# Two graph-attention layers on one core: q's second-layer weights loaded in place through GpSimd, and the first layer's residual loaded one step earlier

## The reference

```python
h = relu(layernorm(x))
q, k, v = h @ Wq + bq, h @ Wk + bk, h @ Wv + bv          # layer 1, 12 heads
p = softmax(where(adj > 0, q @ k.T / sqrt(32) + beta * adj, -9e15))
x = x + p @ v
h = relu(layernorm(x))
q, k, v = h @ Wq1.T, h @ Wk1.T, h @ Wv1.T + bv1          # layer 2
p = softmax(q @ k.T / sqrt(384) + 2 * adj)               # rows of zeros give 0
x = x + (p @ v) @ Wo.T + bo
```

## Time and profile before

| | before |
|---|---|
| median of 3 runs | 1955.08 us (1952.37 to 1955.17) |
| the profiled execution | 1955.73 us, span 1954.0 us |
| TensorE busy | 1900.2 us (97%) |
| VectorE busy | 1819.8 us (93%) |
| ScalarE busy | 1608.5 us (82%) |
| GpSimd busy | 1001.9 us (51%) |
| mean granted TensorE clock | 0.996 |
| chain that ended last | TensorE 63%, VectorE 31% of the span |

### The profile page before, as it was taken

One profiled execution on the slowest core, in us unless ns is written; L12 is line 12 of the kernel. 1 busy time (PEld: TensorE's weight loads), 2 busy tenths in 40 slices (PEclk: granted clock), 3 DMA queues, 4 the chain that ended last, 5 costly groups with the idle time before them and its releaser, 6 DMA issues.

```text
span 1954.0 us, 50144 instructions
## 1 busy us (share of the span) xinstructions
PE 1900.2 (97%) x18396; PEld 1233.7 (63%) x18396; DVE 1819.8 (93%) x3986; ACT 1608.5 (82%) x4150; POOL 1001.9 (51%) x1243
## 2 busy tenths in 40 slices
PE   7999999999999999999999999999999999999999
PEld 5566666666666666666566666666666666666665
DVE  6999999999999999999899999999999999999994
ACT  5899888998988889998878777877778777877785
POOL 6466655566766555665453443434343444344331
PEclk9999999999999999999999999999999999999999
DMA  4888989989989899899887877877887887787774
GB/s 156 210 209 228 224 231 231 236 228 240 229 229 225 230 229 239 230 238 236 219 228 196 215 201 195 212 205 202 203 211 193 214 204 202 203 214 195 202 196 128
DMA packets 104564, 415.94 MB, mean 213 GB/s; under 512 B 27104, under 2 KB 30432, under 8 KB 104320
## 3 DMA queue, kind: packets, MB, share of 16 engines
q1 hardware_dynamic: 77552, 305.11, 64.9%
q0 software_dynamic: 26768, 107.62, 17.3%
HBM read 88.61 MB, written 25.17 MB: 58 GB/s over the span
## 4 chain that ended last, share of the span: by engine, by line
PE 63%; DVE 31%; issue 2%; POOL 1%; ACT 1%; DMA 1%; DVEq 0%; SPq 0%; POOLq 0%
DVE s L432 17%; PE ring L301 15%; PE sc L266 14%; PE out L362 11%; DVE pt L445 11%; PE ring L330 6%; PE ring L283 6%; PE ring L309 5%; PE ring L292 2%; PE ring L332 1%; PE ring L321 1%; DVE stats L491 1%; DVE nmax L432 1%; DMA res<-in_x 0%; DVE oT L483 0%
## 5 line engine op out<-in xcount | busy, mean ns | idle before, releaser
L552 ACT ACTIVATE s<-s,nmax 128x512 f32<-128x512 f32 x1536 | 1095.9, 727 | 197.1 <-DVE nmax L432 196.1
L432 DVE CUSTOM_DVE_ANT_0 s<-sc,bias 128x512 f32<-128x512 f32 x1536 | 968.1, 686 | 57.5 <-PE sc L266 36.0
L445 DVE STREAM_TRANSPOSE pt<-s 128x2048 f32<-128x2048 f32 x285 | 656.9, 2305 | 1.2 <-ACT s L552 1.2
L266 PE MATMUL sc<-k,q 32*128 32x512 f32 x3072 | 439.4, 642 | 39.9 <-DVE nmax L432 36.6
L552 ACT ACTIVATION_READ_ACCUMULATOR s<-s,nmax 128x1 f32 x1536 | 313.2, 204 | 0.0
L362 PE MATMUL out<-pk,v 128*32 128x192 f32 x6080 | 286.5, 329 | 0.0
L362 PEld LDWEIGHTS out<-pk,v 128*32 128x32 f32 x6080 | 178.0, 109 | 135.4 <-issue 98.1
L309 PE MATMUL ring<-wv,hT 128*128 128x384 f32 x1152 | 247.8, 352 | 0.0
L301 PE MATMUL ring<-hT,wq 128*128 128x512 f32 x864 | 243.3, 414 | 3.5 <-DVE hT L460 2.8
L743 POOL TENSOR_TENSOR v<-v,bvx 128x384 f32<-128x384 f32 x64 | 64.6, 1009 | 353.6 <-ACT v L614 353.6
L301 PE MATMUL ring<-hT,wk 128*128 128x512 f32 x864 | 238.7, 415 | 1.0 <-POOL wk L684 1.0
(11 more groups left out here) (98 smaller groups left out, 1916.2 us busy)
## 6 DMA issues: line engine op xcount, KB each, us to landing
pk<-pt SPq DMA_DIRECT2D x1520, 192.0 KB, 4.6
bias<-in_adj POOLq DMA_DIRECT2D x31, 1024.0 KB, 9.4
res<-in_x POOLq DMA_DIRECT2D x16, 768.0 KB, 4.9
x_between<-res POOLq DMA_DIRECT2D x16, 768.0 KB, 5.5
xin<-x_between POOLq DMA_DIRECT2D x16, 768.0 KB, 6.8
res<-x_between POOLq DMA_DIRECT2D x16, 768.0 KB, 5.3
xin<-in_x POOLq DMA_DIRECT2D x15, 768.0 KB, 8.3
out_x<-res POOLq DMA_DIRECT2D x15, 768.0 KB, 3.8
```

Of the source, the lines that this page charges most:

```text
L266: mm = nc.tensor.matmul(m.sc[:, j, :], m.q[rows, s % 2, P * t:P * (t + 1)], m.k[rows, s % 2, :], start=True, stop=True)
L432: nc.vector.tensor_tensor_reduce(out=m.s[:, t % 2, j, :], in0=m.sc[:, j, :], in1=m.bias[g % 2][:, t, :], scale=s_scale[layer], scalar=3.0e ...
L445: nc.vector.transpose(out=to, in_=m.s[:, t % 2].rearrange("p j (i a e) -> p (j i) a e", a=QUADS, e=HD)).then_inc(turned, 1)
L552: nc.scalar.activation(tile, tile, ACT.Exp, bias=m.nmax[s % 2][:, t, j:j + 1], scale=-1.0, accum_out=m.sums[s % 2][:, t, j:j + 1]).then_in ...
```

## The change

It does four things. (1) q's second-layer weight no longer goes through `room` by SyncE's queue during pass 14; GpSimd loads it in place of the old `w[1]` of q at step 6 of pass 15, ahead of k's, when the last q product of that pass is made. (2) ScalarE rounds it at the end of step 7 instead of step 6. (3) GpSimd splits it at step 8 instead of step 7. (4) In the first layer `load_residual` is at step 5 instead of 6.

```diff
-X_STEP, ADJ_STEP, RES_STEP, BIAS_STEPS = 9, (1, 5), (6, 3), (3, 5, 6, 8)
+X_STEP, ADJ_STEP, RES_STEP, BIAS_STEPS = 9, (1, 5), (5, 3), (3, 5, 6, 8)
...
-RELOADS = {(B - 1, 1, 0): 2, (B - 1, 1, 2): 1}
-ROUNDINGS = {(B - 1, 1, 2): 0, (B - 1, 2, 0): 1}
-SPLITS = {(B - 1, 1, 2): 2, (B - 1, 1, 3): 0, (B - 1, 2, 1): 1}
+RELOADS = {(B - 1, 1, 0): (2,), (B - 1, 1, 2): (0, 1)}
+ROUNDINGS = {(B - 1, 1, 3): 0, (B - 1, 2, 0): 1}
+SPLITS = {(B - 1, 1, 2): 2, (B - 1, 2, 0): 0, (B - 1, 2, 1): 1}
...
-                    if (g, c) == (B - 2, 2):
-                        load_weight(1, 0)
...
-                    pool.wait_ge(ready["qk"], nth("qk", B - 1, 2 * DT - 1))
+                    pool.wait_ge(ready["qk"], nth("qk", B - 1, 2 * DT - 2 + n))
...
-                    reload(RELOADS[g, c, t])
+                    for n in RELOADS[g, c, t]:
+                        reload(n)
...
-                    [room[:, 0:DT * D].rearrange("p (t n) -> p t n", t=DT), wk_whole[:], wv_whole[:]])
+                    [w[:] for w in whole])
```

More of the change, by code:

```diff
@@ L904, in __init__ @@
         self.wq, self.wk, self.wv = ([weight(f"{name}{i}", n, i, F32R) for i in range(2)] for n, name in enumerate(("wq", "wk", "wv")))
-        wk_whole, wv_whole = weight("wk_whole", 1, 1, F32), weight("wv_whole", 2, 1, F32)
+        whole = [weight(f"w{name}_whole", n, 1, F32) for n, name in enumerate("qkv")]
         self.wo = sb("wo", [P, DT, D])
```

## The result

The changed kernel takes 1958.19 us (median, 1954.32 to 1962.41) beside 1953.14 us (1949.49 to 1960.11) for the kernel before, in runs on the same chip. The ratio is 1.0022, with a 95% interval of 1.0012 to 1.0033, which is 2.3 to 6.4 us slower.

What follows compares the result with a forecast made beforehand. The prediction took a TensorE-VectorE chain as the bound, with TensorE waiting at the change of layers; +1.0, -0.97 and -1.52 gave -1.5 us, so 1954.2 profiled and 1953.6 us median, range 1950.0 to 1957.0.

Steps and rivals of the forecast that it cites:

- The residual in the other passes costs nothing: First layer's steady passes: loading the residual one step earlier changes nothing in 14 passes of 56.0 us.
- GpSimd's chain: Change of layers: GpSimd runs 3.3 us earlier, so TensorE's waits for k's split (0.97 us) and `ksum` (1.52 us) go.
- The load took 903.14 to 912.73 ... by that row it lands near 902.2: Residual's load at the change of layers: issued near 892.6, taking 9.6 us as before, so GpSimd's 6.10 us wait goes.
- so I take the middle of the upper half, some 8 us: no wait: q's weight, issued at 897.5 and wanted by ScalarE at 907.5: lands after some 8 us, so ScalarE does not wait.
- q's weight is late: Rival at ScalarE's rounding: load takes 11 us or more, giving 1954.6 us at 11.0; chance 0.14, shared with a late chain.
- Forecast -1.5: TensorE at the change of layers: q's product +1.0, k's product -0.97, sums item -1.52, together -1.5 us.
- another case: Rival on GpSimd: its chain stays late for another reason, 1955.1 to 1956 us; chance 0.14, shared with q's weight late.
- The rounding's +1.0 us: ScalarE's moved rounding of q delays the copy freeing q's buffer; TensorE's wait before q's product grows from 0.77 to 1.8 us.
- A fall's price: TensorE's clock after a gap: a fall to its lower level costs 1.6 us.
- Its chance of 0.18: Rival: one more fall of TensorE's clock, possibly behind the 1.8 us gap before q's product, giving 1955.2 us; chance 0.18.
- The 0.05 for slower: Whole kernel: chance 0.05 of being slower by over 0.2%, against 0.84 for no measurable change and 0.11 for faster.
- moves late or two mishaps at once: What slower by over 0.2% required: chunk 0's moves delayed above 5 us (1959.6 us), or two mishaps together; chance 0.05.

Runs made afterwards that it cites:

- e6: Changed kernel with q's load issued by GpSimd ahead of v's split instead of behind it; 1956.87 us, ratio to the kernel before 1.0017.
- e5: Changed kernel with q's load issued by SyncE's queue instead of by GpSimd; 1959.44 us, ratio to the kernel before 1.0032.
- e11: Changed kernel with q's rounding on GpSimd at step 8 instead of ScalarE at step 7; 1957.57 us, ratio to the kernel before 1.0018.
- e2: Changed kernel with the residual's load put back from step 5 to step 6; 1960.27 us, ratio to the kernel before 1.0036.
- e9: Changed kernel whose residual load of pass 15 brings one of four row tiles, 192 of 768 KB; 1955.09 us, ratio to the kernel before 1.0008.
- e7: Kernel before with the residual at step 3 and q's rounding and split at the changed places, q's weight loaded early; 1955.42 us, ratio to before 1.0017.
- e3: Changed kernel with the first layer's residual loaded at step 3 instead of 5; 1955.74 us, ratio to the kernel before 1.0012.
- e8: Kernel before with the residual at step 3 and k's rounding on GpSimd instead of ScalarE; 1951.4 us, ratio to the kernel before 0.999.
- e12: Kernel before with the residual at step 5 and q's and k's roundings both on GpSimd; 1950.08 us, ratio to the kernel before 0.9986.
- e10: Kernel before with the residual at step 5 and k's rounding on GpSimd instead of ScalarE; 1950.84 us, ratio to the kernel before 0.9985.
- e1: Kernel before with only the first layer's residual moved, loaded at step 5 instead of 6; 1952.92 us, ratio to the kernel before 0.9998.

## Why the prediction was wrong

- **The residual in the other passes costs nothing: right.** 56.0 us a pass before and after.
- **GpSimd's chain: right for its followers, wrong at its head.** k's split and `ksum` wait for nobody any more (928.94 and 939.73). But GpSimd still stood for v's weight (3.13 us), the residual (3.06, since it landed near 906.2 in before's frame, which is 5.0 us earlier, and not at 902.2) and ScalarE's rounding (2.54), and k's split came at 920.85, not near 913. In before's frame that is 915.8, 0.6 us sooner than before, not 3.3. It sufficed only because TensorE itself was late by then.
- **The step that failed: "The load took 903.14 to 912.73 ... by that row it lands near 902.2", and "so I take the middle of the upper half, some 8 us: no wait".** Each load was priced by the row of a load like it in the old program. There q's load (issued 876.50, 11.0 us) was over when v's went out (886.98), and k's (900.97) and the residual's (903.14) came after v's had landed; now v's, q's, k's weight and the residual, 2.5 MB, share DMA engines whose share was already 1.04 in 891 to 894. q's weight landed 909.5 in before's frame, 12 us after the issue I had forecast, where 8 was the term and 11.5 the point at which the gain is gone. The issue was 2.8 us late (905.33, which is 900.3 in that frame, for 897.5), because v's weight took 9.5 us and not 6.5, and the load then took 9.1 us; but an issue 4.3 us earlier (e6) brought the landing only 0.2 us forward. The residual took 13.7 us and not 9.6. e5, e6 and e11 (earlier issue, no earlier landing), e2 and e9 (fewer bytes ahead, 3.3 and 3.6 us sooner) show that it is the bytes, each by one profiled execution.
- **"q's weight is late" was a rival, with the right mechanism and a price too small.** It gave 1954.6 us at 11.0 us and the whole gain gone at 11.5. The price counted only q's own wait beyond its due time. What it left out: ScalarE works in order and waits for k's weight as well (1.13 us); both waits stand ahead of the copy that frees q's buffer, so they add up in TensorE's wait, 6.22 - 1.8 = 4.4 us more, against 3.36 + 1.13 = 4.5; and a wait of that length brings a fall of the clock, 1.5 us. Forecast -1.5, plus 4.5, plus 1.5 makes +4.5 us, of 4.9 in the distance. Of the 3.36 us some 1.4 are there because ScalarE came to the rounding early: it was free 58.7 us after the transposes of pass 14, where it was at 60.1 before (907.51), since this execution has no fall near 891. Its chance of 0.14, shared with another case, was too low too, since the trace showed a full stretch.
- **The rounding's +1.0 us: right**, 1.83 us in e7 against 1.8, and 178.0 us against 177.1 in the distance.
- **A fall's price: right**, 1.5 us at 923.09 for 1.6. Its chance of 0.18 was given for a gap of 1.8 us. The wait that came was over 4 us, and behind all five such waits (after, e2, e3, e5, e11) the clock fell.
- **The chances and the range.** The 0.05 for slower rested on "moves late or two mishaps at once". The two mishaps were one: the late load makes the gap, and the gap makes the fall.

## What to carry to other kernels

When loads are moved into a stretch where the DMA engines are full, price them together: add up all bytes wanted there, divide by the GB/s that the windows show, and lay the landings out one behind the other; no load keeps the landing time of its old row. A staging buffer that lets a load go out 24 us early (29.1 for 52.9 us after the transposes of pass 14), ahead of the crowd, can be worth more than the memory it takes. Put the operation that waits for a late load on an engine with idle time and nothing urgent behind it: on an in-order engine that others wait for, such waits were handed on nearly whole. All operations of this kind have to move: with q's alone moved (e11), k's took its place.

## What the runs showed of the hardware

- The time from issue to landing of a 576 KB load went from 4.3 us (k's, before) to 13.7 us (q's by SyncE in e5) and 17.1 us (q's into `room` in e8). One and the same load, v's, in programs that are the same up to its landing, took 5.9, 7.6 and 10.0 us (e12, e10, e1). With the share near 1.0, an issue 4.3 us earlier brought the landing 0.2 us forward (e6).
- TensorE's clock fell behind all five waits of over 4 us before q's product (after, e2, e3, e5, e11), for 1.5 to 2.7 us. It fell behind 3.45 (e6), 2.65 (e8) and 1.83 us (e7) as well, for 1.5 to 1.6 us, and not behind 2.98 (e1), 2.00 (e3) or 1.96 us (e9). So the length of a wait alone does not tell it. The gaps of 1.6 to 1.9 us near 890 and 955 were followed by a fall in some executions and not in others of kernels that are the same there.
- The opening takes up to 7 us more in one execution than in another (61.4 to 68.5 us to the same instruction), more than the effect that was to be measured. Between before and after some 2.4 of the 5.3 us are a fall of the clock behind a gap that both have; what makes the rest was not looked into.
